# Attention with experts on one core: dividing, stacking and projecting the heads by pairs, and a shorter combine spread one step to a chunk

## The reference: what is computed

```python
def _L0_attn_ref(x, gamma, w_qkv, w_out):
    normed = x / l2 * dim ** 0.5 * gamma
    q, k, v = split of (normed @ w_qkv), 16 heads of 64
    attn = softmax(causal(q * d ** -0.5 @ k.T))
    return (attn @ v) joined over heads @ w_out
def _L0_ffn_ref(tgt, ...):
    router_w = softmax over the top 2 of (tgt @ Wr.T + br)
    h = relu(tgt @ W1[e].T + b1[e]);  o = h @ W2[e].T + b2[e]
    return layer_norm(tgt + sum_e router_w * o, gamma, beta)
return x + _L0_attn_ref(xn, ...) + _L0_ffn_ref(xn, ...)
```

## Time and profile before

| what | value |
|---|---|
| median of 3 runs | 1462.79 us (1461.44 to 1465.05) |
| the profiled execution, its own time | 1463.13 us |
| its span, first to last instruction | 1461.4 us |
| mean granted TensorE clock | 0.958 |

### The profile page before, as it was taken

The page is one execution under the profiler, slowest core; times in us unless marked ns, Lnnn a source line. Parts: engine busy times, 40 slices in busy tenths (PEclk is TensorE's granted clock), DMA queues, the critical chain, the costliest instruction groups (busy, mean ns, idle before and its releaser), DMA issues.

```text
span 1461.4 us, 27770 instructions
## 1 busy us (share of the span) xinstructions
PE 1351.4 (92%) x8360; PEld 1124.9 (77%) x8361; DVE 1038.1 (71%) x2674; ACT 947.8 (65%) x2094; POOL 867.2 (59%) x1304
## 2 busy tenths in 40 slices
PE   4569998999879999999999899899899999899998
PEld 4446666999757888788788788788788788788886
DVE  5656654222257788888888888888888888888773
ACT  2435544555447677677777677677677777677775
POOL 3426651332227568667667667767766766766666
PEclk9669999999869999999999999999999999999999
DMA  6222221222122022112112212112212212211112
GB/s 204 89 60 63 63 54 55 77 75 77 47 57 52 3 41 50 29 30 51 35 33 44 43 30 46 38 36 42 41 30 46 42 32 39 48 30 32 30 30 59
DMA packets 131078, 72.47 MB, mean 50 GB/s; under 512 B 80216, under 2 KB 116864, under 8 KB 130944
## 3 DMA queue, kind: packets, MB, share of 16 engines
q1 hardware_dynamic: 114304, 54.18, 18.2%
q0 software_dynamic: 4096, 8.40, 1.9%
q10 hardware_dynamic: 12544, 8.29, 1.9%
HBM read 20.47 MB, written 16.52 MB: 25 GB/s over the span
## 4 chain that ended last, share of the span: by engine, by line
PE 53%; DVE 11%; issue 5%; ACT 2%; DMA 1%; SPq 0%; DVEq 0%; POOLq 0%; ACTq 0%
PE max_ps L1281 8%; PE score_ps L1299 6%; PE score_ps L1298 6%; PE misc_ps L1341 6%; PE head_ps L1318 5%; PE head_ps L1327 5%; PE head_ps L1325 5%; PE head_ps L1323 5%; DVE max_ps L1140 4%; PE misc_ps L1262 3%; DVE x_row L1156 2%; PE misc_ps L1256 2%; DVE q_a L1126 1%; PE misc_ps L1257 1%; PE misc_ps L1258 1%
## 5 line engine op out<-in xcount | busy, mean ns | idle before, releaser
L1032 POOL TENSOR_TENSOR p_lo<-probs,p_hi 128x512 fp32r<-128x512 f32 (+3 forms) x560 | 536.1, 958 | 188.5 <-ACT p_hi L1084 183.9
L1082 ACT ACTIVATE probs<-score_ps 128x512 f32<-128x512 f32 (+3 forms) x768 | 377.5, 492 | 257.0 <-PE score_ps L1299 243.8
L1140 DVE CUSTOM_DVE_ANT_0 max_ps<-max_ps,mask 128x128 f32<-128x128 f32 (+7 forms) x512 | 390.7, 763 | 111.1 <-PE max_ps L1281 87.8
L1298 PE MATMUL score_ps<-q_a,k_a 128*128 128x512 f32 (+3 forms) x768 | 304.3, 396 | 0.2 <-ACT p_hi L1084 0.2
L1281 PE MATMUL max_ps<-k_a,q_a 128*128 128x512 f32 (+3 forms) x768 | 238.6, 366 | 54.2 <-DVE shift L1140 45.0
L1024 POOL TENSOR_SCALAR_AFFINE_SELECT probs<-probs 128x128 f32<-128x128 f32 x512 | 153.7, 300 | 202.3 <-ACT p_hi L1084 136.9
L1299 PE MATMUL score_ps<-q_b,k_b 65*128 65x512 f32 (+3 forms) x768 | 269.6, 351 | 0.0
L1084 ACT ACTIVATE p_hi<-score_ps 128x512 fp32r<-128x512 f32 (+3 forms) x560 | 263.1, 470 | 0.0
L1318 PE MATMUL head_ps<-probs,v_all 128*65 128x128 f32 (+3 forms) x1088 | 248.7, 310 | 0.0
L1281 PEld LDWEIGHTS max_ps<-k_a,q_a 128*128 128x128 f32 x768 | 140.8, 195 | 114.9 <-DVE shift L1140 86.5
L1323 PE MATMUL head_ps<-p_hi,v_hi 128*65 128x512 f32 (+3 forms) x560 | 210.3, 376 | 0.0
(11 more groups left out here) (165 smaller groups left out, 2086.6 us busy)
## 6 DMA issues: line engine op xcount, KB each, us to landing
k_a<-k_a SPq DMA_DIRECT2D x64, 256.0 KB
q_b<-q_a SPq DMA_DIRECT2D x64, 256.0 KB
q_b<-shift SPq DMA_DIRECT2D x512, 0.5 KB
sorted_x<-zeros SPq DMA_DIRECT2D x13, 384.0 KB, 5.0
rows<-sorted_x SPq DMA_DIRECT2D x39, 128.0 KB, 2.1
sorted_y<-result ACTq DMA_DIRECT2D x39, 128.0 KB, 1.8
acc<-in_L_attn_x_dram SPq DMA_DIRECT2D x4, 512.0 KB, 7.2
x_row<-in_L_attn_x_dram SPq DMA_DIRECT2D x8, 256.0 KB
```

The costliest lines, as they stand in the source:

```text
L1032: pool.tensor_tensor(p_lo[:, lo_slot(g, c), w0:w1], probs[:, slot, w0:w1], p_hi[:, slot, w0:w1].bitcast(F32), ALU.subtract).then_inc(pool_ ...
L1082: ins = act.activation(probs[:, slot, 0:width], src[:, 0:width], ACT.Exp, scale=SCALE)
L1140: dve.tensor_tensor_reduce(out=max_ps[:, at:at + width], in0=max_ps[:, at:at + width], in1=mask[:, SEQ - width:SEQ], scale=-1.0, scalar=-M ...
L1298: pe.matmul(dst, k_a[i][s][:, keys], q_a[i][s][:, qs], start=True, stop=False)
```

## The change

Both attention stages get a new way from `head_ps` to `acc`, and the combine is rewritten. By parts:

1. **Division before the projection.** ScalarE copies `head_ps` to `raw` (65 rows, a ring of two units). SyncE moves its row 64 (the sums, 1024 numbers) to 128 partitions x 8 (`sums`), VectorE inverts them there, SyncE moves them back into row 64 (`inverse`), and a third DMA, `spread`, copies that one row to 64 partitions (`rden_all`, 256 KB, the source being one partition read 64 times). VectorE then multiplies (`normalise`, two instructions of 64 x 512 per unit) into `stacked`, head 0 of the pair in partitions 0 to 63 and head 1 in 64 to 127. For unit W - 1 the sums move at chunk 5 of unit W, are inverted at 8 and move back at 10; for unit W - 2 the row is spread at chunk 0 of unit W and multiplied at chunks 3 and 4. `raw` of that unit must be free before ScalarE's copy at chunk 7.
2. **One projection for a pair.** `project_pair` multiplies `stacked` (128 rows) by `wo` (128 x 128): 8 tiles a pair, at chunks 7 and 9 of odd units, added by two VectorE instructions of 128 x 512. The last pair of each stage keeps the old form (`last_y`).
3. **v from rounded parts.** The v projection becomes three matmuls of rounded operands per tile in place of one full float32 one. `nT` is then not needed after `routing`.
4. **Combine.** 33 steps in place of 45: `center` moves to ScalarE (chunks 7 to 10 of the group's unit 2), `norm`, `gamma`, `beta`, `add` become two `scalar_tensor_tensor`, and `beta` is added once to all of `acc` by GpSimd in `experts` (8 instructions of 128 x 512). The 33 steps stand at chunks 0, 2, 4, 5, 7, 9, 11 of units 3 to 6 and at 0, 2, 4, 5, 7 of unit 7.
5. **Start and end of a stage.** q and k are projected for the first 512 tokens first, the SBUF copies go by halves (8 of 128 KB), and the first unit begins its scores after tiles 0 to 3 of the maximum; tiles 4 to 7 follow at its chunks 0 and 1. The last store goes in smaller pieces. The loads of the next q, k, v weights are issued earlier.

```diff
-            wo = sb(ph2, "wo", [HEAD + 1, 2, D + 1])
+            raw = sb(ph2, "raw", [HEAD + 1, 2, SEQ])
+            sums = sb(ph2, "sums", [P, 2, TILES])
+            inverse = sb(ph2, "inverse", [P, 2, TILES])
+            rden_all = sb(ph2, "rden_all", [HEAD, SEQ])
+            stacked = sb(ph2, "stacked", [P, SEQ])
...
-            COMBINE = ([("center", q) for q in range(GROUP)]
-                       + [("first", q) for q in range(GROUP)] + [("second", q) for q in range(GROUP)]
+            COMBINE = ([("first", q) for q in range(GROUP)] + [("second", q) for q in range(GROUP)]
                        + [("stats", q) for q in range(GROUP)] + [("aggr", 0), ("var", 0)]
                        + [("rsqrt", n) for n in range(RSQRT_STEPS)]
-                       + [(kind, q) for kind in ("norm", "gamma") for q in range(GROUP)]
-                       + [(kind, q) for q in range(GROUP) for kind in ("beta", "add")])
-            COMBINE_AT = [(2, c) for c in (2, 4, 5, 6)]
-            COMBINE_AT += [(g, c) for g in (3, 5) for c in (0, 0, 1, 2, 3, 4, 5, 5, 6, 7, 8, 9, 11, 11)]
-            COMBINE_AT += [(7, c) for c in (0, 0, 1, 2, 3, 3, 3, 4, 4, 5, 5, 7, 7)]
+                       + [(kind, q) for q in range(GROUP) for kind in ("gamma", "add")])
+            COMBINE_AT = [(g, c) for g in (3, 4, 5, 6) for c in (0, 2, 4, 5, 7, 9, 11)]
+            COMBINE_AT += [(7, c) for c in (0, 2, 4, 5, 7)]
+            CENTRE_AT = [(2, c) for c in (7, 8, 9, 10)]
-            Y_AT = [7, 9, 11]
+            Y_AT = {7: 0, 9: 1}
...
+                    if stacks(W - 1):
+                        order += [(kind, W - 1, 0) for kind, at in (("sums", 5), ("invert", 8), ("inverse", 10))
+                                  if at == c]
+                    if stacks(W - 2):
+                        order += [(kind, W - 2, n) for kind, n, at in (("spread", 0, 0), ("norm", 0, 3),
+                                                                      ("norm", 1, 4)) if at == c]
...
+                        if kind == "spread":
+                            W = g
+                            sp.wait_ge(inverse_moved[W % 2], n_spread(W) * 16)
+                            if W > W0:
+                                sp.wait_ge(norm_done, 2 * n_stacked(W - 1) + 2)
+                            sp.dma_start(rden_all[:],
+                                         raw[HEAD:HEAD + 1, W % 2].unsqueeze(1).broadcast_to([1, HEAD, SEQ])).then_inc(spread[W % 2], 16)
...
+                            if half == 0 and W - W0 >= 2:
+                                act.wait_ge(norm_done, 2 * n_stacked(W - 2) + 2)
                             act.wait_ge(pv_done, n_chunk(W, c) + 1 + RING)
...
+                    def normalise(W, half):
+                        s, cols = W % 2, slice(half * BANK, (half + 1) * BANK)
+                        rows = slice(s * HEAD, (s + 1) * HEAD)
+                        if half == 0:
+                            dve.wait_ge(spread[s], n_spread(W) * 16)
+                            if s == 0 and W // 2 > Q0:
+                                dve.wait_ge(misc_ready, place[("y", W // 2 - 1, 1)] + 1)
+                        dve.tensor_tensor(stacked[rows, cols], raw[0:HEAD, s, cols], rden_all[:, cols],
+                                          ALU.mult).then_inc(norm_done, 1)
...
+                                pe.matmul(part, nT_hi[:, t0:t0 + P], wqkv_hi[:, 2], start=True, stop=False)
+                                pe.matmul(part, nT_hi[:, t0:t0 + P], wqkv_lo[:, 2], start=False, stop=False)
+                                ins = pe.matmul(part, nT_lo[:, t0:t0 + P], wqkv_hi[:, 2], start=False, stop=True)
```

More of the change, by code:

```diff
@@ L694, in attention_and_experts @@
         pool_split = sem("pool_split")
[L695 removed]
+        copies_done = [sem(f"copies_done{i}") for i in range(2)]
         shift_done = [sem(f"shift_done{i}") for i in range(2)]
@@ L1225, in _ @@
-                    run(walk, dve)
+                    w_lo(hps[0])
+                    combined, y_so_far = 0, added0
+                    for o in order:
+                        kind, g, c = o
+                        if kind == "max":
+                            maximum(g, c)
+                        elif kind == "project_lo":
+                            project(g, c)
+                        elif kind == "weights":
+                            w_lo(g)
+                        elif kind == "invert":
+                            invert(g)
+                        elif kind == "add":
+                            after_combine(combined)
+                            add_y(g, c)
+                            y_so_far = added[("y", g, c)]
+                        elif kind == "last_y":
+                            last_y(g, c)
+                        elif kind == "last_add":
+                            after_combine(combined)
+                            add_last_y(g, c)
+                        elif kind == "combine":
+                            if COMBINE[g][0] == "add" and y_so_far > added0:
+                                dve.wait_ge(y_added, y_so_far)
+                            combine(c, g)
+                            combined = c * COMBINE_STEPS + g + 1
+                        if o[0] == "norm":
+                            normalise(o[1], o[2])
```

676 lines of the change are left out of this document (342 added, 334 removed).

## The result

The changed kernel takes 1817.55 us (median of 4 runs, 1813.76 to 1820.42), the kernel before 1462.12 on the same chips (1459.07 to 1465.05). The ratio is 1.243, its 95% interval 1.2392 to 1.2468. The forecast was 1421, with a range of 1385 to 1650: wrong in sign, and the time lies above the range. What came is rival (a), the spread that lands late, and dearer than it was priced (about 1680).

A forecast was written before the change was run, and what follows sets the result against it. The prediction took TensorE as the bound in plain units, with VectorE and GpSimd adding combine cost. Sum: 1463.1 - 8 (pairs) - 22 (combine) - 10 (starts) - 2 (first stage's pairs, last store) = 1421 us; range 1385 to 1650.

The forecast's parts named there:

- rival (a): Attention units: the spread lands late, VectorE then TensorE wait, units of about 22 and 22.5 us, about 1680 us; chance 0.28.
- I take the near row for the forecast: Spread transfer: priced like the copies over 64 partitions, 1.4 us plus some 2 for landing; the other bound was 89 us.
- 0.06 apart ... I take the first, since the nearest row has loads of the same width: v projection, odd units: 24 matmuls 0.06 us apart take 1.44, gaining 0.36; second case 0.11 apart, 2.64, losing 0.84.
- The even unit: Last attention stage: TensorE's 16.1 us plus waits of 1.04 and 0.8 behind normalise give 18.0 us.
- GpSimd's part: VectorE's normalise: GpSimd delays each of the two by 0.4 us, together 0.8 in an even unit.
- Rival (c): Even units: VectorE is not the limit, TensorE alone counts, about 1358 us; chance 0.10.
- rival (b): Each normalise waits for a whole p_lo, 1.3 us; pairs take 37.7 us, the kernel about 1510; chance 0.08.
- The pairs: Last attention stage: 34.5 us a pair against 34.8, - 0.3 x 28 pairs = - 8 us.
- The combine: Combine groups: excess of 4.9 us a group against 7.7, - 2.8 x 8 groups = - 22 us.
- odd units 3, 5, 7 take the steps in slack: 0.6 together: Combine groups: steps in these odd units fit VectorE's slack and cost 0.6 us a group together.
- The starts: Starts of both attention stages: working by halves gains 5 us each, - 10 together, bounds 0 and - 18.
- Beta: GpSimd's beta adds in experts cost nothing, covered by an 18.2 us wait; without that cover, 10 us once.

The follow-up runs named there:

- the run with the wide source: Changed kernel with the spread copying the 64 partitions of raw to rden_all, so nothing is divided: 1489.95 us (one run).
- the run with half the rows: Changed kernel with the spread writing 32 of 64 partitions (128 KB), the others holding 1.0: 1524.03 us (one run).
- with one row: Changed kernel with the spread writing 1 partition (4 KB), the other 63 of rden_all holding 1.0: 1483.35 us, ratio 1.0153 to the kernel before.
- The run with two products: Changed kernel with the spread read from a DRAM row (1487.6 us), v's product with the low weights left out: 1463.94 us, ratio 1.0014.

## Why the prediction was wrong

**The spread.** The step that failed is the choice in rival (a), "I take the near row for the forecast". The forecast had 8.3 us in even and 6 in odd units until VectorE comes to `normalise`, and took 1.4 + 2 for the spread; the transfer is 10.3, and 11.9 pass from issue to use. The near row was near in bytes and in the shape of the destination, but far in the one thing that counted here: 64 source partitions (1489.95 us for the whole kernel in the run with the wide source) against one (1817.55). The earlier trace rows already had the hint, half the partitions at half the rate, 188 GB/s against 387. That the geometric middle of the bounds, 11 us, lies so close is luck: nothing in the case says that the truth is in the middle. The trace has 27 GB/s in the row at 870.40, and the same in the run with half the rows.

**What rival (a) mis-sized.** It gave units of 22 and 22.5 us; they take 22.7 and 25.1. TensorE's waits were forecast at 3.1 and 4.0 and are 4.5 and 4.6. In the odd unit TensorE has 17.9 us of work, not 16.5 (v, below). The clock costs more: TensorE's busy time is 18.17 and 20.23 against 16.81 and 17.90 with one row, 1.4 and 2.3 us, at a granted clock of 0.92 and 0.86 against 1.00. Together 13.0 a pair instead of 9.7, 92 us in 28 pairs. The first stage, where rival (a) has nothing, adds 33. That the combine hides in the idle time was right (62 us of it, where rival (a) took 40). Its 11.2 us from issue to use left out the 2 us for landing that the forecast had counted; measured are 11.9 from issue to use less 10.3 for the transfer, 1.6.

**v.** "0.06 apart ... I take the first, since the nearest row has loads of the same width": 0.11 apart. That is the 2.64 of the prediction's second case, + 0.84 in place of - 0.36 in an odd unit, 1.2 us a pair and 34 in all; the prediction named the number under what would show it wrong. The run with two products measured it. The step that failed is to read the price of a run of 24 off the distance within one pair.

**The even unit** was forecast at 18.0 with one wait for the maximum, and is 17.7 with one wait of 0.9. The mechanism held, `normalise` in front of tile 5. That the sum came so close is partly luck: the waiting was forecast at 1.84 and is 0.9, and TensorE's busy time was forecast at 16.1 and is 16.81. Why it falls by 1.1 us and not by the 1.79 of its 16 instructions is open. GpSimd's part was less: `normalise` took 0.83 on average, 0.14 over its length alone and not 0.4. In that run all 38 of its 120 instructions that took over 0.9 us began while a `p_lo` was running; the longest took 1.64. The two runs that moved it did not win this part by placing. Rival (c), that VectorE isn't the limit, falls with the wait of 0.9, and rival (b), that each `normalise` waits for a whole `p_lo`, with the 0.83.

**The pairs** come to 35.6 instead of 34.5: without the spread's cost the stacking gives + 0.8 x 28 = + 22 us, not - 8.

**The combine** was forecast at - 22. By itself it gave - 29; in the stacked kernel its excess was 112.7 less three pairs of 35.6, 5.9 a group, - 14 in all. The step "odd units 3, 5, 7 take the steps in slack: 0.6 together" failed there: unit 3 alone costs 3.8 in the group shown, since the gathers land late. Unit 2 takes 17.1 us where it took 22.1, so they have less time; that this is why they are late was not tested. No run shows the 0.7 to 1.4 us that the forecast adds to GpSimd in unit 2 behind `normalise`: in the run with one row GpSimd is busy 16.1 of that unit's 17.1 us (window 811.60:828.70), where the forecast had 19.3. The 1.5 us each for the even units 4 and 6, with four steps before tile 5, was too dear for the old frame, where they cost 0.65 and 0.4.

**The starts** were forecast at - 10 and cost + 20. In the run with one row the first stage's first exponential comes 7.7 us sooner, and the last stage's first score 10 us sooner after the experts' last matmul. But the first units are 13.5 and 14.2 us longer, of which about 6 each are SyncE's queue, and the expert stage ends 10 us later by beta: - 7.7 - 10 + 10 + 13.5 + 14.2 = + 20. "SyncE gets three more DMAs a unit ... costs nothing" held for those three. It passed over the copies, which the halving moves in front of four shifts. The other part of the longer first unit is not a loss: with the order of the queue put right, or with all maxima ahead, the last stage's first unit ends at the same time within 0.4 us. From these ends (444.8, and 439.5 before) less beta's 10, the two starts without SyncE's mistake give about - 5 us together, half of the forecast: an estimate from the profiled executions.

**Beta** was forecast free and costs 9 us. The prediction had the price: "without that cover they would cost 10 us once". What it didn't ask is when the load is issued.

**The account.** From the forecast: 1421, + 334 for the spread, + 30 for the pairs, + 30 for the starts with beta in them, + 8 for the combine in this frame, 1823, against 1817.6 (the other pairs of the first stage are 3 us shorter).

## What to carry to other kernels

Price a DMA that leaves SBUF by the partitions that it reads from, not by its bytes alone: here a row that was to reach 64 partitions got there faster by way of DRAM (1.4 us for 256 KB, behind a write of 4 KB that had time) than out of one SBUF partition (10.3). Price a run of small matmuls by a run of such matmuls (0.11 us each), not by one pair (0.06). An engine's idle time covers a new task only from the moment at which that task's data has landed (beta's landed at 292.3, as the idle time ended, and cost 9 us), so ask when its load is issued and behind what; the same holds for the gathers that a moved step has to wait for. And put off-path work of an in-order engine into the stretches where that engine has room: here, the same 33 steps were worth 4.5 us more in odd units.

## What the runs showed of the hardware

- While the spread out of one partition is under way (window 870.40:880.00), the mean busy share of the 16 DMA engines is 0.93 at 27 GB/s, and SyncE's issues behind it take longer: in the even unit before the one shown, one `q_b<-q_a` issue lasts 3.15 us and one `k_a<-k_a` 2.29, where others take 0.6. Of the 128 `q_b<-q_a` issues 29 last over 1.5 us in the changed kernel, none in the run with one row.
- The DRAM row read 64 times cost no more than 64 different partitions: medians of 0.16 and 0.31 us for a 4 KB packet.
- The rounded matmuls of v, 128 columns with a weight load each, start 0.11 us apart at a granted clock of 1.00 and 0.21 at 0.50.
- With a wait of 4.6 us (878.8 to 883.3) the granted clock is 0.50 from 881.00 to 887.80. With one wait of 0.9 us (the plain pair of the run with one row) it stayed at 1.00.
